# Attention on one core: the maximum products of a key tile as four row tiles in four banks, reduced in one instruction, and the row of maxima placed in the sums' bank

## The reference

```python
scores = jnp.einsum('bqhd,bkhd->bhqk', q, k) / np.sqrt(hd).astype(np.float32)   # 8 x 16 heads, 1024 x 1024, hd = 32
attn = jax.nn.softmax(scores, axis=-1)
out = jnp.einsum('bhqk,bkhd->bqhd', attn, v).reshape(B, L, D)
```

## Time and profile before

| | us |
|---|---|
| median of 3 runs | 5264.52 (5264.1 to 5265.49) |
| the profiled execution | 5257.78 |
| its span | 5255.9 |
| TensorE matmuls busy | 4717.2 (90%) |
| VectorE busy | 3750.7 (71%) |
| GpSimd busy | 2560.1 (49%) |
| ScalarE busy | 2358.7 (45%) |
| mean granted TensorE clock of the run | 0.965 |

### The profile page before, as it was taken

One profiled execution on the slowest core, in us unless ns is written; L12 is line 12 of the kernel. 1 busy time (PEld: TensorE's weight loads), 2 busy tenths in 40 slices (PEclk: granted clock), 3 DMA queues, 4 the chain that ended last, 5 costly groups with the idle time before them and its releaser, 6 DMA issues. The chain is left out here.

```text
span 5255.9 us, 83572 instructions
## 1 busy us (share of the span) xinstructions
PE 4717.2 (90%) x25792; PEld 3011.7 (57%) x25792; DVE 3750.7 (71%) x5321; ACT 2358.7 (45%) x3683; POOL 2560.1 (49%) x1341
## 2 busy tenths in 40 slices
PE   6689999968888799999999999999996775999999
PEld 6678888846666433333333333333333664888888
DVE  6667777667787677777777777777774886677776
ACT  4433333322222255565656556565653343333332
POOL 2334444345565455555555555555554554344443
PEclk9999999989999799999999999999997886999999
DMA  4465555334444422222222232222214554555552
GB/s 136 139 198 179 172 176 161 119 135 159 153 144 140 133 51 64 63 64 64 64 58 57 63 64 64 62 64 64 64 37 129 169 160 139 177 178 168 173 175 91
DMA packets 431929, 613.85 MB, mean 117 GB/s; under 512 B 188288, under 2 KB 189568, under 8 KB 431808
## 3 DMA queue, kind: packets, MB, share of 16 engines
q1 hardware_dynamic: 390848, 545.67, 36.8%
q0 software_dynamic: 40960, 66.65, 4.0%
HBM read 452.44 MB, written 178.33 MB: 120 GB/s over the span
## 5 line engine op out<-in xcount | busy, mean ns | idle before, releaser
L1468 POOL TENSOR_TENSOR att_pairsum<-att_p,att_p 128x1024 f32<-128x1024 f32 x512 | 1203.1, 2369 | 994.5 <-ACT att_p L1486 994.5
L1540 DVE TENSOR_REDUCE att_halves<-att_mx 128x2 f32<-128x1024 f32 x1024 | 1211.2, 1221 | 534.3 <-PE att_mx L1579 531.1
L1486 ACT ACTIVATE att_p<-att_st 128x512 f32<-128x512 f32 x2048 | 1183.5, 597 | 869.1 <-PE att_st L1601 831.2
L1601 PE MATMUL att_st<-att_q,att_k 128*128 128x512 f32 x2048 | 960.3, 494 | 48.0 <-ACT att_p L1486 46.5
L1601 PEld LDWEIGHTS att_st<-att_q,att_k 128*128 128x128 f32 x2048 | 372.7, 187 | 825.7 <-issue 409.3
L1611 PE MATMUL att_op<-att_p,att_v 128*32 128x512 f32 x4096 | 549.0, 608 | 1.1 <-ACT att_p L1486 1.0
L1579 PE MATMUL att_mx<-att_k,att_q 32*128 32x512 f32 x2048 | 520.0, 503 | 27.7 <-DMA att_v<-v 15.1
L845 DVE TENSOR_TENSOR e_w<-e_raw,e_w 128x2048 fp32r<-128x2048 f32 x192 | 439.3, 2290 | 10.0 <-ACT e_w L840 6.1
L863 ACT ACTIVATE e_sg<-e_gp 128x324 f32<-128x324 f32 x256 | 113.3, 443 | 630.9 <-PE e_up L176 630.9
L840 ACT ACTIVATE e_w<-e_raw 128x2048 fp32r<-128x2048 f32 x192 | 366.4, 1909 | 56.1 <-DMA e_raw<-in_w_gate 48.1
L899 DVE SCALAR_TENSOR_TENSOR e_xg<-e_yp,e_meta,e_xg 108x512 f32<-108x512 f32 x192 | 144.2, 751 | 314.9 <-PE e_yp L176 314.9
(11 more groups left out here) (147 smaller groups left out, 9176.0 us busy)
## 6 DMA issues: line engine op xcount, KB each, us to landing
e_raw<-in_w_gate SPq DMA_DIRECT2D x64, 1024.0 KB, 5.6
e_raw<-in_w_up SPq DMA_DIRECT2D x64, 1024.0 KB, 9.5
e_raw<-in_w_down SPq DMA_DIRECT2D x64, 1024.0 KB, 5.8
att_q<-q SPq DMA_DIRECT2D x192, 256.0 KB, 4.1
att_k<-k SPq DMA_DIRECT2D x256, 128.0 KB, 5.8
r_x<-in_x SPq DMA_DIRECT2D x16, 1024.0 KB, 6.0
x<-r_base SPq DMA_DIRECT2D x16, 1024.0 KB, 9.4
qkv_x<-x SPq DMA_DIRECT2D x16, 1024.0 KB, 5.6
```

The costliest lines, as they stand in the source:

```text
L1468: nc.gpsimd.tensor_tensor(out=pairsum[h][g % 2][:, :], in0=pr[h][2 * g % RING][:, :], in1=pr[h][(2 * g + 1) % RING][:, :], op=ALU.add).the ...
L1486: nc.scalar.activation(pr[h][kt % RING][:, c * HALF:(c + 1) * HALF], st[c][:, :], ACT.Exp, scale=SCALE).then_inc(s_exp, 1)
L1540: nc.vector.tensor_reduce(out=halves[:, n // 2, n % 2, :], in_=mx[n % 2][:, :, :], axis=AX.X, op=ALU.max).then_inc(s_max, 1)
L1601: nc.tensor.matmul(st[c][:, :], kst[b][:, h, kt * P:(kt + 1) * P], qst[b][:, h, c * HALF:(c + 1) * HALF], start=True, stop=True).then_inc( ...
```

## The change

- Each pair's main parts of q and k are loaded a second time, into new tiles: `mq` holds q of both heads twice (partitions 0 to 63 and 64 to 127), `mk` the first half of the keys at 0 to 63 and the second at 64 to 127. The main k at L1422 comes by three DMAs of 256 KB in place of five. So a pair has eleven DMAs, and 2560 KB in place of 1792 KB.
- `rough` takes one query tile with all keys: four matmuls on the four row tiles, into the four banks of the only `mx` buffer. It waits for the reduction before it. There are 8 calls a pair, one in each stage: the last three for the next pair in kt 0 to 2, the first five for the pair after next in kt 3 to 7.
- `maxima` is one reduction of 128 x 2048 to 128 x 2 a query tile, 8 a pair. The greater of two halves falls away, and the cast to bf16 is a `tensor_tensor` maximum of `big` with itself. The split is thus two operations.
- `row` writes four column tiles of the bank `zp`, in kt 4 (ROW), behind the products and ahead of score 2. It waits for z's copy of the pair before. Each row copy is two instructions of 32 x 512 columns. ScalarE's stand behind the third exponential of kt 4, VectorE's behind the first reduction of the pair after next.
- The totals of a pair move from kt 4 and 6 to kt 5 and 6, and the first waits for the row copies. z's copy moves from behind exponential 0 of kt 3 to behind exponential 2 of kt 2.

```diff
-    NM = 2 * KT
-    ROUGH = ((1, 1, 1), (1, 0, 1), (1, 1, 1), (1, 0, 1), (1, 1, 1), (0, 0, 0), (0, 0, 1), (1, 0, 1))
-    TURN = KT - 2
+    TURN = 3
+    ROW = TURN + 1
+    FIRST = KT - TURN
+        mq = [sb(f"mq{b}", [P, L], F32R) for b in range(DEPTH)]
+        mk = [sb(f"mk{b}", [P, HALF], F32R) for b in range(DEPTH)]
-        mx = S.pair(ps, "mx", [P, 2, HALF])
+        mx = ps("mx", [P, 2, 2, HALF])
...
+                for c in range(2):
+                    rows = slice(2 * c * HD, 2 * (c + 1) * HD)
+                    sp.dma_start(mq[b][rows, :].bitcast(F32), q_in[0, src[0], :]).then_inc(s_in[b], 16)
+                    sp.dma_start(mk[b][rows, :].bitcast(F32), k_in[0, src[0], half(c)]).then_inc(s_in[b], 16)
...
-                        if last and (kt, x) == (3, 0):
+                        if last and (kt, x) == (2, 2):
                             copy_z(*last)
-                        if left and (kt, x) == (TURN, 3):
+                        if left and (kt, x) == (ROW, 2):
                             copy_row(*ahead(i, b, 1))
...
+            def maxima(i, b, qt):
+                p = DEPTH * i + b
+                dve.wait_ge(s_mx, KT * p + qt + 1)
+                if qt == 0:
+                    dve.wait_ge(s_mlo, p)
+                nc.vector.tensor_reduce(out=big[:, :, qt], in_=mx[:, :, :, :].rearrange("p h c k -> p h (c k)"),
+                                        axis=AX.X, op=ALU.max).then_inc(s_max, 1)
+            def split(i, b):
+                p = DEPTH * i + b
+                dve.wait_ge(s_max, KT * (p + 1))
+                dve.wait_ge(s_row, p)
+                nc.vector.tensor_tensor(out=parts[:, :, :, 0], in0=big[:, :, :], in1=big[:, :, :],
+                                        op=ALU.max).then_inc(s_mhi, 1)
                 dve.wait_ge(s_mhi, p + 1)
                 nc.vector.tensor_tensor(out=parts[:, :, :, 1], in0=big[:, :, :], in1=parts[:, :, :, 0],
                                         op=ALU.subtract).then_inc(s_mlo, 1)
+            def copy_row(i, b):
+                dve.wait_ge(s_row, DEPTH * i + b + 1)
+                for c in range(2):
+                    nc.vector.tensor_copy(qst[b][3 * HD:4 * HD, 0, half(c)], zp[tile(0, c), :]).then_inc(s_rowq[0], 1)
             def step(i, b, left):
                 if left:
-                    maxima(*ahead(i, b, 1))
+                    for qt in range(FIRST, KT):
+                        maxima(*ahead(i, b, 1), qt)
+                    split(*ahead(i, b, 1))
+                for qt in range(FIRST):
+                    if left >= 2:
+                        maxima(*ahead(i, b, 2), qt)
+                    if left and qt == ROW - TURN - 1:
+                        copy_row(*ahead(i, b, 1))
...
-            def rough(i, b, n):
+            def rough(i, b, qt):
                 p = DEPTH * i + b
-                qt, c = n // 2, n % 2
-                if n == 0:
+                if qt == 0:
                     pe.wait_ge(s_in[b], 16 * N_IN * (i + 1))
-                pe.wait_ge(s_max, past(NM * p + n - 1))
-                for h in range(2):
-                    last = nc.tensor.matmul(mx[n % 2][:, h, :], qst[b][h * HD:(h + 1) * HD, h, qt * P:(qt + 1) * P],
-                                            kst[b][h * HD:(h + 1) * HD, h, c * HALF:(c + 1) * HALF],
-                                            start=True, stop=True)
+                pe.wait_ge(s_max, KT * p + qt)
+                for c in range(2):
+                    for h in range(2):
+                        rows = slice((2 * c + h) * HD, (2 * c + h + 1) * HD)
+                        last = nc.tensor.matmul(mx[:, h, c, :], mq[b][rows, qt * P:(qt + 1) * P], mk[b][rows, :],
+                                                start=True, stop=True)
                 last.then_inc(s_mx, 1)
...
-            def totals(p, g):
+            def totals(p, g, left):
                 if g == 0:
                     pe.wait_ge(s_zo, p)
+                    for h in range(2):
+                        pe.wait_ge(s_rowq[h], 2 * (p + (2 if left else 1)))
...
+                    if kt == ROW and left:
+                        row(*nxt)
+                    if kt in (ROW + 1, ROW + 2):
+                        totals(p, kt - ROW - 1, left)
+                    for x in (2, 3):
+                        scores(p, b, kt, x)
+                    if kt < TURN and left:
+                        rough(*nxt, FIRST + kt)
+                    if kt >= TURN and left >= 2:
+                        rough(*ahead(i, b, 2), kt - TURN)
+                    for x in (0, 1):
+                        if kt + 1 < KT:
+                            scores(p, b, kt + 1, x)
```

More of the change, by code:

```diff
@@ L1397, in attention, with tile, half @@
         N_OUT = 4
-        N_IN = 3 + 5 + 1
-        KBLK = ((0, 1, 0), (1, 0, 0))
+        N_IN = 3 + 3 + 2 + 2 + 1
+        def tile(h, c):
+            return slice((2 * h + c) * HD, (2 * h + c + 1) * HD)
+        def half(c):
+            return slice(c * HALF, (c + 1) * HALF)
         def ahead(i, b, k):
@@ L1586, in row @@
                 p = DEPTH * i + b
-                pe.wait_ge(s_max, NM * (p + 1))
+                pe.wait_ge(s_mhi, p + 1)
                 pe.wait_ge(s_mlo, p + 1)
-                for qt in range(KT):
+                pe.wait_ge(s_zo, past(p - 1))
+                for t in range(KT // 2):
                     for h in range(2):
-                        last = nc.tensor.matmul(
-                            mx[1][(3 - h) * HD:(4 - h) * HD, qt // (KT // 2), qt % (KT // 2) * P:(qt % (KT // 2) + 1) * P],
-                            parts[:, h, qt, :], identb[:, :], start=True, stop=True)
+                        for c in range(2):
+                            last = nc.tensor.matmul(zp[tile(h, c), t * P:(t + 1) * P], parts[:, h, c * (KT // 2) + t, :],
+                                                    identb[:, :], start=True, stop=True)
                 last.then_inc(s_row, 1)
@@ L1610, in products @@
                     for c in range(2):
-                        last = nc.tensor.matmul(op[(2 * h + c) * HD:(2 * h + c + 1) * HD, :], v[b][:, kt, h, :],
-                                                pr[h][kt % RING][:, c * HALF:(c + 1) * HALF],
+                        last = nc.tensor.matmul(op[tile(h, c), :], v[b][:, kt, h, :], pr[h][kt % RING][:, half(c)],
                                                 start=kt == 0, stop=kt == KT - 1)
                 last.then_inc(s_v, 1)
-            def totals(p, g):
+            def totals(p, g, left):
                 pe.wait_ge(s_add, 2 * (NG2 * p + g) + 2)
@@ L1620, in totals @@
                     pe.wait_ge(s_zo, p)
+                    for h in range(2):
+                        pe.wait_ge(s_rowq[h], 2 * (p + (2 if left else 1)))
                 for h in range(2):
                     for c in range(2):
-                        last = nc.tensor.matmul(zp[(2 * h + c) * HD:(2 * h + c + 1) * HD, :], ones[:, :],
-                                                pairsum[h][g % 2][:, c * HALF:(c + 1) * HALF],
+                        last = nc.tensor.matmul(zp[tile(h, c), :], ones[:, :], pairsum[h][g % 2][:, half(c)],
                                                 start=g == 0, stop=g == NG2 - 1)
@@ L1640, in step @@
                     if kt in (0, 2) and before:
[L1641 to L1650, removed]
-                        elif left:
[L1652 to L1664, removed]
+                        totals(p - 1, 2 + kt // 2, left)
+                    if kt == ROW and left:
[11 more added lines that the diff above has]
+                            scores(p, b, kt + 1, x)
+                        elif left:
+                            scores(p + 1, nxt[1], 0, x)
+            for qt in range(KT):
+                rough(0, 0, qt)
             row(0, 0)
-            for n in range(FIRST):
-                rough(0, 1, n)
+            for qt in range(FIRST):
+                rough(0, 1, qt)
             for x in range(2):
```

49 lines of the change are left out of this document (15 added, 34 removed).

## The result

The changed kernel takes 5297.85 us (median of 5 runs, 5289.11 to 5298.74) against 5264.1 before (again 5 runs): ratio 1.0063, 95% interval 1.005 to 1.0075. It is slower by 0.6%, clear of the noise, and outside the range of 5110 to 5285. The profiled execution has a span of 5296.9 us, 41.0 more than before.

The account below looks back on a forecast made before the run. TensorE was taken to set the pace, ScalarE close behind. Pairs 1.0 us shorter, x 62 = -61, plus 16 at the start, gave -45: 5264.5 to 5220 us; own range 5185 to 5255, with rivals 5110 to 5285.

Parts of the forecast that it names:

- Pace, and the insertion that hides: TensorE sets the pace; a plain stage's insertion frees the next score at +2.09 us, before ScalarE does at +2.27.
- B: Rival, chance 0.10: four row tiles don't stream together, each insertion takes 0.65 us more, 1.6 a pair, total 5317.
- VectorE: Eight reductions a pair of 2.29 us, begun 0.54 behind their matmuls, done before the next insertion asks, 0.36 to spare.
- The held split: VectorE's two split operations wait for GpSimd's sums of kt3; kt4's row goes at +2.5 us instead of +1.0.
- A: Rival, chance 0.24: the split's first operation goes ahead of GpSimd's sum, row on time, a pair 31.3 us, total 5125.
- Stage lengths without the clock: kt0 to kt7 take 4.52, 3.18, 4.52, 3.18, 6.1, 4.04, 4.04, 3.18 us: 32.8 a pair against 33.77.
- rival C: Chance 0.08: TensorE, idling more, falls to 1.2 GHz for a time each pair, or rises later at the start; 5240 up.
- no second price: kt4's insertion waits to 4.7 us for a reduction, but frees the next score at 5.2, before ScalarE does (5.7).
- The start: Start adds 16 us (8 to 24): loads +4, eight rounds +6, scores behind the row +10, first pair gains some 4.
- The term given as "about 14.5": At the start, time from the row to the first scores, with five insertions ahead: about 14.5 us against 4.3.

Follow-up runs that it names:

- the first experiment: Changed kernel, with GpSimd's first sum of kt3 waiting until VectorE's split is done: 5105.23 us, ratio 0.9706.
- the one with the copies alone: Changed kernel with ScalarE's three copies moved (o behind exponential 1 of kt0, z exponential 1 of kt3, row exponential 3 of kt4): 5243.5 us.
- the one with the reduction first: Changed kernel with two buffers for the maxima and VectorE's first reduction of the pair after next ahead of the split: 5353.76 us, ratio 1.0187.

## Why the prediction was wrong

- **Pace, and the insertion that hides: right.** The four maximum matmuls last 0.51 us together, their weights 0.19. The score behind them waited for ScalarE. B is out.
- **VectorE: right.** Reductions of 2.293 us, begun 0.56 behind the matmuls (2605.49 - 2604.93); outside kt4 only kt7's insertion comes close to waiting.
- **The held split: right** (medians of the 64 pairs 2298 and 2273 ns). GpSimd was ahead by 0.18 us, not 0.07 (2607.82 - 2607.64). So A, at 0.24, was less likely than I gave it. The two runs that put the row on time by unlike means agree to 4 us. The prediction's account of it, two SBUF inputs, leaves out that the cast of one input was held in the same way.
- **Stage lengths without the clock: right.** kt3, kt4 on: 3.10, 6.66, 5.19, 3.95, 3.17, 4.44, 3.10, 4.45, for 3.18, 6.1, 4.04, 4.04, 3.18, 4.52, 3.18, 4.52. In the changed kernel every pair has a fall; in the two kernels closest to it, each with matmuls added, pairs without one took 32.57 and 32.84. The forecast was 32.8. Within kt4 one term was too small: I took ScalarE's row copies at 0.49 us each, but the next exponential starts 2615.25 - 2613.39 = 1.86 behind the last, 0.4 more than three steps of 0.49.
- **The clock: the step that failed.** It was rival C, at 0.08, set aside because "the last pair, 22.9 of 27 us busy, stayed at 1.00". That share was an average over evenly spread pauses of about 0.5 us. The change puts 1.50 and 1.28 us of idle time within 3.9 us (2611.02 to 2614.87), and the clock falls to 1.2 GHz behind them in each pair. The walk had both idle times, but the second at no price, because the scores behind it waited for ScalarE anyway ("no second price"); with the second alone left, the clock fell in 15 of 17 pairs. A fall costs 1.6 to 1.7 us, pairs with one against pairs without in the same kernel: 0.3 in kt4 (products 0.72 behind the last score, 0.43 at the full clock) and about 1.2 in kt5 (5.19 for 3.95 of kt6, the same work). Against the pairs of 34.15 us here that is an estimated 62 x (34.15 - 32.57) = 98 or 62 x (34.15 - 32.84) = 81 us: without it the kernel would be near 5200 to 5217, and my 5220 stood on the right mechanism with this term missing.
- **The start: +12 for +16.** The three parts came to 21.3 for 20; the first pair gave back 9.6 for 4. The term given as "about 14.5" adds up to 14.1; measured were 14.7 from the row to the scores.
- **The range.** It left C out above 5285, although I had found a stall of 1.5 us in each pair. It should have carried the price of half a clock behind a stall on its upper side.

**Open:** the third idle time alone brings the clock down in three pairs of four in one kernel (2611.22 to 2614.08) and in 2 of 18 in another (the first experiment's rows), and the rows from the row matmuls on are alike. What else takes part was not settled. One thing that the traces show and no run tested: in the changed kernel the falls start at 2308.55, 2342.68, 2376.81, 2410.95, and so on, 34.13 us apart from 1864.81 to 3981.08, although single pairs take 33.85 to 34.49 us. In the two closest kernels they are also 34.13 us apart, or 68.27 where a pair has none, with one exception of 98.99. So a fall seems to come only at set times, and an idle time brings one where it lies right for such a time.

## What to carry to other kernels

When a change shortens the engine that sets the pace, price each stall it leaves twice: its own length, and the half clock that may follow on TensorE. Look at how the idle time is bunched, not at its share. A VectorE operation of two SBUF inputs beside GpSimd additions can cost a whole addition, even at 16 elements: put it ahead of the addition with a wait, or write it as a reduction of one input (a cast of one input was held too). And a copy of ScalarE between two exponentials that a matmul waits for costs its full length: the three moved to where ScalarE had slack gave 2.4 us a pair (31.08 to 28.69).

## What the runs showed that I had not expected

- A fall of the clock held on after TensorE was full again: it lasted 3.4 us in most kernels, mostly 6.8 in the one with the copies alone, 3.4 to 10.2 in the one with the reduction first.
- Where it came in nearly every pair, the pairs were of nearly one length, 34.0 to 34.1 us on average, whatever they held: 32.57 or 32.84 us without a fall, and with the copies alone 31.3, as long as every pair had its fall of 6.8 us. So filling idle time with work moved neither the pair nor the total, until the falls went, and then 150 us went at once (5292.93 to 5140.3), half of it the copy's place.
- Four more loads a pair, DMA share 0.29 to 0.40, cost nothing in the middle, and nothing measurable in all (ratio 1.0007, interval 0.9997 to 1.0016).
